# Attention kernel: both pairs of maximum products of a step issued together, behind the products of values

## The chip, the cores and the metric

The program runs on one core of a Trainium2 chip. The metric is the device time of one execution in microseconds (us), lower is better. In this text PE is TensorE's matmul stream and PEld its weight loads, DVE is VectorE, ACT ScalarE, POOL GpSimd, SP the queue engine that issues most DMAs.

## The reference

Four images of 32 x 32 tokens with 192 channels pass through two blocks. Each block adds an attention over an image's 1024 tokens (12 heads of 16 channels, with bias terms from relative positions), then a feed-forward part (routed experts in the first block; a small attention over tokens, an MLP and four experts in the second). What the change touches is the softmax attention, of which the kernel has three of the same size:

```python
attn = einsum('bnqd,bnkd->bnqk', q, k) * scale + bias     # 48 (image, head) pairs, 1024 x 1024
attn = softmax(attn, axis=-1)
out  = einsum('bnqk,bnkd->bnqd', attn, v)
```

The first two (stages c0 and c1) have the bias, the third (f1) has none.

## The kernel before, in words

`attention` (line 525) is called three times. It works through 24 pairs of heads (two heads of one image side by side), and for each pair through 8 steps, one for each tile of 128 keys. It computes scores with the keys on the partitions, so that the exponential's output can be the right operand of the product with the values. The maximum over the keys, which keeps the exponential in range, is therefore found ahead of time, by separate products with the queries on the partitions, and enters the scores as one more row of the operands. So TensorE issues, for each step of a pair:

- **scores** (`score`, line 692, matmuls at L703): for both heads, a tile of 128 keys against 1024 queries, in two matmuls of 512 columns each, into the PSUM tensors s0 and s1. ACT takes each with one exponential of 128x1024 (L996). The scores that PE issues in step n are those of key tile n; in the eighth step they are tile 0 of the next pair.
- **weigh** (line 707, matmuls at L716), the products of values, for the key tile of the step before: eight matmul records of float32, in four column groups of the array, accumulated over the eight steps in one bank. It needs the two exponentials of that tile, and these are the same two that the scores ahead of it have waited for.
- **maxima** (`use_bank`, line 660, matmuls at L688), the maximum products, for pairs ahead: four a step, as two pairs (one product of each head; the two heads lie on different rows of the array). I call the two pairs of a step A and B. Each product fills a bank of 128x512, which DVE reduces to one column (`dve_max`, L750). There are 32 products for each pair of heads; 54 are issued before the loop, the rest by a written-out plan.

Once a pair, ahead of A in step 4, stands the **row** product (L681): after the last of the 32 reductions DVE makes the negated maxima in two small operations (L755, L759), TensorE transposes them, ACT copies them out (L763), and SP's DMAs (`place_rows`, line 633) put them in place for the pair's scores.

The maximum products use three PSUM banks in turn. A product of an even number waits for both banks of its pair to be free, that is, for the reductions of the products three and two uses before it; the last of these is the first product of the previous pair. The wait and the plan are these lines:

```python
                banks = (pos, pos + 1) if item[1] % 2 == 0 else ()
            for before in (b - 3 for b in banks):
                ...
                    pe.wait_ge(*free(USES[before], pair if before >= 0 else pair - 1))
...
        for step in range(1, KT + 1):
            PLAN.append([[items.pop(0) for _ in range(2)] for _ in range(2)])
            if step == ROWS + 1:
                PLAN[-1][0].insert(0, (1, "row"))
```

The eight banks of PSUM are spent: four for the scores, three for the maxima, one for the sums. All waits are written by hand, in each engine's own stream; there is no scheduler. ACT's order is the exponentials of both heads of a tile, with the copy of the maximum row behind the first exponential of tile 4 and the copy of the sums (L1002) behind tile 0. An exponential of tile n waits for the weigh of tile n-2. In the last turn of pairs the maxima that no pair is left for are skipped: pair 22 (counted from 0) has only the first ten, pair 23 none.

Of the kernel before, what the change touches and what calls it, by code (L numbers as in the profile page):

```python
# [524 lines left out]
def attention(nc, name, vt, rel, scratch, hot, ident16, by_pool, res, wo, bo, stats=None, room=None, spots=None, spare=None,  # L525
# [6 lines left out]
    with Pool(nc, name) as m:  # L532
# [48 lines left out]
        def queries(h, version, first, count):  # L581
            at = (h * versions + version) * L + first
            return slice(at, at + count)
# [76 lines left out]
        def use_bank(pe, pair, pos, item, u, skip=()):  # L660


            started = pair is None
            g = pos if started else len(START) + len(USES) * u + pos
            if item[1] == "row":
                banks = (pos,)
            else:
                banks = (pos, pos + 1) if item[1] % 2 == 0 else ()
            for before in (b - 3 for b in banks):
                if started:  # L670
                    if before >= 0:
                        pe.wait_ge(*free(START[before], 0))
                else:
                    while before >= 0 and USES[before][0] in skip:
                        before -= 3
                    pe.wait_ge(*free(USES[before], pair if before >= 0 else pair - 1))
            bank, q = mps[g % 3], 0 if started else pair
            v = (u + item[0]) % RING
            if item[1] == "row":
                pe.wait_ge(s_m16, q + (item[0] + 1))  # L680
                ins = pe.matmul(bank[0:2 * KT, 0:P], m16[:, :], ident16, start=True, stop=True)  # L681
                ins.then_inc(s_row, 1)
            else:
                n = item[1]
                h, qi, c = n % 2, n // 4, n // 2 % 2
                rows = slice(64 * h, 64 * h + RANK)
                q0 = (c if rel else 0) * L + qi * P
                ins = pe.matmul(bank[:, :], qm[v][rows, q0:q0 + P], km[v][rows, c * CHUNK:(c + 1) * CHUNK],  # L688
                                start=True, stop=True)
                ins.then_inc(s_mm, 1)  # L690

        def score(pe, pair, u, h, kt, first=False):

            if kt == 0:
                pe.wait_ge(s_at[0], (pair + 1) * 32)
            if not first:
                pe.wait_ge(s_e, pair * 16 + (2 * kt + h - 1))
            version = kt * P // Q if rel else 0
            if rel and kt == Q // P:
                pe.wait_ge(s_at[1], (pair + 1) * (32 * (versions - 1)))  # L700
            kcol = slice(h * L + kt * P, h * L + (kt + 1) * P)
            for c in range(2):
                ins = pe.matmul(sps[h][:, c * CHUNK:(c + 1) * CHUNK], ka[u][0:R_END, kcol],  # L703
                                qa[u][0:R_END, queries(h, version, c * CHUNK, CHUNK)], start=True, stop=True)
            ins.then_inc(s_s, 1)

        def weigh(pe, pair, u, kt):

            pe.wait_ge(s_e, pair * 16 + (2 * kt + 2))
            if kt == 0:  # L710
                pe.wait_ge(s_vs, pair * 2 + 2)
                pe.wait_ge(s_o, pair + 1)
            for h in range(2):
                for c in range(2):
                    row = 32 * (2 * h + c)
                    ins = pe.matmul(ops[row:row + 32, :], vs[u][:, (h * KT + kt) * 32:(h * KT + kt + 1) * 32],  # L716
                                    pr[h][kt % 2][:, c * CHUNK:(c + 1) * CHUNK], start=kt == 0, stop=kt == KT - 1)
            ins.then_inc(s_pv, 1)

        def pe_pair(pe, turn, pair, u, skip=()):  # L720

            pos = 0

            def maxima(steps):
                nonlocal pos
                for item in steps:
                    if item[0] not in skip:
                        if item == (2, 0):
                            pe.wait_ge(s_lm[(u + 2) % RING], (turn + (u + 2) // RING + 1) * (16 * MAX_LOADS) + CONST)
                        use_bank(pe, pair, pos, item, u, skip)  # L730
                    pos += 1

            for step in range(1, KT + 1):
                if step < KT:
                    for h in range(2):
                        score(pe, pair, u, h, step)
                elif 1 not in skip:
                    pe.wait_ge(s_ld[(u + 1) % RING], (turn + (u + 1) // RING + 1) * (16 * LOADS) + CONST)
                    for h in range(2):
                        score(pe, pair + 1, (u + 1) % RING, h, 0)  # L740
                maxima(PLAN[step - 1][0])
                weigh(pe, pair, u, step - 1)
                maxima(PLAN[step - 1][1])

        def bank_of(u, item):
# [114 lines left out]
        with nc.Block() as block:  # L860
# [72 lines left out]
            @block.tensor  # L933
            def _(pe):
                pe.wait_ge(s_ones, ONES)
                pe.wait_ge(s_lm[0], 16 * MAX_LOADS + CONST)
                for pos, item in enumerate(START):
                    if item == (1, 0):
                        pe.wait_ge(s_lm[1], 16 * MAX_LOADS + CONST)
                    use_bank(pe, None, pos, item, 0)  # L940
                pe.wait_ge(s_ld[0], 16 * LOADS + CONST)
                score(pe, 0, 0, 0, 0, first=True)
                score(pe, 0, 0, 1, 0, first=True)
                with pe.Fori(0, LAST) as it:
                    for u in range(RING):
                        pe_pair(pe, it, it * RING + u, u)
                for u in range(RING):
                    pe_pair(pe, LAST, LAST * RING + u, u, LATE[u])
                project(pe)
# [1300 lines left out]
```

## Time and profile before

| | us |
|---|---|
| runs shown, median of 3 | 3374.49 |
| lowest and highest | 3373.45, 3380.55 |
| the profiled execution, its own time | 3370.78 |
| its span, first to last instruction | 3368.9 |
| PE busy in the span | 2764.8 (82%) |
| DVE busy | 2414.6 (72%) |
| ACT busy | 1860.7 (55%) |

The span and the execution's own time differ by 1.9 us. The three attentions' loops fill roughly 240 to 767, 1434 to 1961 and 2190 to 2707 us of the span; the rest is normalization, projections and feed-forward. Busy time of PE counts from a matmul's start to its modelled end, so that overlapping matmuls hide gaps in the issue; to read how closely TensorE's work follows itself, start times are compared instead.

### The profile page before, as it was taken

How to read it: one execution, taken by the hardware profiler on the slowest of the kernel's cores; microseconds unless marked ns; L12 is line 12 of the kernel's file. 1: busy time of each engine (PE TensorE's matmuls, PEld its weight loads, DVE VectorE, ACT ScalarE, POOL GpSimd, SP SyncE). 2: the span in 40 equal slices, each digit the busy share in tenths (PEclk: the TensorE clock that was granted, in tenths of full speed). 3: DMA queues.
4: the chain of work that ended last, by engine and by line, in shares of the span. 5: the costliest groups of instructions: out<-in, count | busy, mean ns of one | idle time of the engine just before them, and what ended most of it. 6: DMA issues, size and time to landing. Idle time of an engine off the chain costs nothing. (4 is left out here: it accounts for less than half of the span.)

```text
span 3368.9 us, 62705 instructions
## 1 busy us (share of the span) xinstructions
PE 2764.8 (82%) x18708; PEld 1277.7 (38%) x18708; DVE 2414.6 (72%) x4597; ACT 1860.7 (55%) x2592; POOL 435.2 (13%) x513
## 2 busy tenths in 40 slices
PE   5948999997499239589999956199999959599999
PEld 3612222226499126222222234022222236366666
DVE  6458999974766354579999955589999835465665
ACT  4416777773255124167777736067777736465554
POOL 0010111111333510101111110201111100000000
PEclk9759999996699667599999977599999979699999
DMA  2555776664122214567766701101111110200000
GB/s 64 169 125 114 151 148 142 148 126 143 33 78 76 70 31 146 134 110 150 149 146 149 145 22 50 57 28 52 48 48 49 48 32 1 55 22 5 9 5 14
DMA packets 202070, 277.27 MB, mean 82 GB/s; under 512 B 54302, under 2 KB 93454, under 8 KB 201930
## 3 DMA queue, kind: packets, MB, share of 16 engines
q1 hardware_dynamic: 162346, 211.32, 27.1%
q0 software_dynamic: 19920, 31.57, 4.0%
q10 hardware_dynamic: 19664, 32.60, 3.3%
q8 instruction: 77, 1.26, 0.2%
q14 instruction: 63, 0.52, 0.1%
HBM read 196.93 MB, written 77.46 MB: 81 GB/s over the span
## 5 line engine op out<-in xcount | busy, mean ns | idle before, releaser
L750 DVE TENSOR_REDUCE c1att_mx<-c1att_m 128x1 f32<-128x512 f32 x768 | 493.4, 685 | 35.7 <-PE c1att_m L688 30.6
L750 DVE TENSOR_REDUCE c0att_mx<-c0att_m 128x1 f32<-128x512 f32 x768 | 493.4, 685 | 32.5 <-PE c0att_m L688 27.2
L750 DVE TENSOR_REDUCE f1att_mx<-f1att_m 128x1 f32<-128x512 f32 x768 | 493.3, 685 | 26.5 <-PE f1att_m L688 21.8
L996 ACT ACTIVATE c1att_p<-c1att_s 128x1024 f32<-128x1024 f32 x384 | 373.9, 1020 | 152.0 <-PE c1att_s L703 151.9
L996 ACT ACTIVATE c0att_p<-c0att_s 128x1024 f32<-128x1024 f32 x384 | 373.9, 1020 | 148.8 <-PE c0att_s L703 148.7
L996 ACT ACTIVATE f1att_p<-f1att_s 128x1024 f32<-128x1024 f32 x384 | 373.9, 1020 | 143.8 <-PE f1att_s L703 142.8
L1426 ACT ACTIVATE moe_h<-moe_u,moe_bu 128x512 f32<-128x512 f32 x192 | 136.5, 711 | 175.6 <-PE moe_u L1343 93.9
L688 PE MATMUL f1att_m<-f1att_km,f1att_qm 16*128 16x512 f16 x768 | 155.7, 401 | 88.6 <-DVE f1att_ka L959 52.9
L716 PE MATMUL f1att_o<-f1att_p,f1att_vs 128*32 128x512 f32 x1536 | 206.2, 609 | 0.6 <-ACT f1att_p L996 0.6
L716 PE MATMUL c0att_o<-c0att_p,c0att_vs 128*32 128x512 f32 x1536 | 206.2, 609 | 0.6 <-ACT c0att_p L996 0.6
L716 PE MATMUL c1att_o<-c1att_p,c1att_vs 128*32 128x512 f32 x1536 | 206.1, 609 | 0.6 <-ACT c1att_p L996 0.6
L688 PE MATMUL c1att_m<-c1att_km,c1att_qm 64*128 64x512 f16 x768 | 156.2, 402 | 58.0 <-DVE c1att_mx L750 35.0
L688 PE MATMUL c0att_m<-c0att_km,c0att_qm 64*128 64x512 f16 x768 | 156.3, 403 | 57.7 <-DVE c0att_mx L750 34.8
L703 PE MATMUL f1att_s<-f1att_qa,f1att_ka 113*128 113x512 f16 x768 | 202.7, 385 | 0.8 <-ACT f1att_p L996 0.4
L1356 PE MATMUL moe_y<-moe_dh,xt 128*128 128x192 f16 x1536 | 195.1, 246 | 0.0
L1463 DVE TENSOR_TENSOR xt<-moe_h,xt 128x512 f16<-128x512 f32 x192 | 131.3, 691 | 86.3 <-ACT xt L1428 85.3
L1356 PE MATMUL moe_y<-moe_dl,xt 128*128 128x192 f16 x768 | 188.9, 246 | 0.0
L688 PEld LDWEIGHTS f1att_m<-f1att_km,f1att_qm 16*128 16x128 f16 x768 | 37.3, 92 | 322.6 <-DVE f1att_mx L750 264.3
L688 PEld LDWEIGHTS c1att_m<-c1att_km,c1att_qm 64*128 64x128 f16 x768 | 37.8, 93 | 292.3 <-DVE c1att_mx L750 262.4
L688 PEld LDWEIGHTS c0att_m<-c0att_km,c0att_qm 64*128 64x128 f16 x768 | 37.8, 93 | 291.7 <-DVE c0att_mx L750 262.2
L703 PE MATMUL c1att_s<-xt,c1att_ka 113*128 113x512 f16 x512 | 135.7, 387 | 7.6 <-DMA xt<-c1att_mrow 7.1
L1356 PEld LDWEIGHTS moe_y<-moe_dh,xt 128*128 128x128 f16 x1536 | 139.0, 98 | 3.7
(608 smaller groups left out, 5430.8 us busy)
## 6 DMA issues: line engine op xcount, KB each, us to landing
xt<-rel_parts SPq DMA_DIRECT2D x256, 128.0 KB, 5.0
xt<-qk_parts SPq DMA_DIRECT2D x192, 128.0 KB, 4.4
y<-rel_parts SPq DMA_DIRECT2D x128, 128.0 KB, 5.6
y<-qk_parts SPq DMA_DIRECT2D x96, 128.0 KB, 5.1
c0att_qm<-rel_parts SPq DMA_DIRECT2D x144, 64.0 KB, 2.1
c1att_qm<-rel_parts SPq DMA_DIRECT2D x144, 64.0 KB, 2.1
expert_rows<-y SPq DMA_DIRECT2D x39, 192.0 KB, 2.0
o_sums<-c0att_o ACTq DMA_DIRECT2D x24, 256.0 KB, 4.3
```

The costliest lines, as they stand in the source:

```text
L688: ins = pe.matmul(bank[:, :], qm[v][rows, q0:q0 + P], km[v][rows, c * CHUNK:(c + 1) * CHUNK], start=True, stop=True)
L703: ins = pe.matmul(sps[h][:, c * CHUNK:(c + 1) * CHUNK], ka[u][0:R_END, kcol], qa[u][0:R_END, queries(h, version, c * CHUNK, CHUNK)], start ...
L716: ins = pe.matmul(ops[row:row + 32, :], vs[u][:, (h * KT + kt) * 32:(h * KT + kt + 1) * 32], pr[h][kt % 2][:, c * CHUNK:(c + 1) * CHUNK], ...
L750: dve.tensor_reduce(mx[:, n:n + 1], bank[:, :], AX.X, ALU.max).then_inc(s_mx, 1)
L996: act.activation(pr[h][kt % 2][:, :], sps[h][:, :], ACT.Exp).then_inc(s_e, 1)
L1356: ins = pe.matmul(yps[q % 2][t // 2][:, (t % 2) * C:(t % 2 + 1) * C], hidden[q % 2][:, x], down[:, w], start=k == 0 and i == 0, stop=k == ...
L1426: act.activation(h32[:, i % 2 * CHUNK:(i % 2 + 1) * CHUNK], bank[:, :], ACT.Gelu, bias=bias, scale=1.0 / W_SCALE).then_inc(s_h32, 1)
L1463: dve.tensor_tensor(hl[q % 2][:, cols], h32[:, i * CHUNK:(i + 1) * CHUNK], hh[q % 2][:, cols], ALU.subtract).then_inc(s_hl, 1)
```

## The change

The change swaps two lines of `pe_pair`. Before, a step's order on TensorE was scores, A, weigh, B; now it is scores, weigh, A, B. In step 4 the row product, which belongs to A's list, moves behind weigh with it. No instruction is added or removed, and no wait's value changes.

```diff
@@ -738,8 +738,8 @@
                     pe.wait_ge(s_ld[(u + 1) % RING], (turn + (u + 1) // RING + 1) * (16 * LOADS) + CONST)
                     for h in range(2):
                         score(pe, pair + 1, (u + 1) % RING, h, 0)
+                weigh(pe, pair, u, step - 1)
                 maxima(PLAN[step - 1][0])
-                weigh(pe, pair, u, step - 1)
                 maxima(PLAN[step - 1][1])
```

## Rows read from the trace of the kernel before

**Rows 1.** Stretches of c0's and f1's steady loops: length, busy times, granted clock, DMA share, GB/s
```profile
276.20:742.00 465.80, 452.68 (x2770) 114.80 (x2768) 448.38 (x735) 346.01 (x386) 63.73 (x94) 1.00 0.68 142
...
2201.00:2684.00 483.00, 469.27 (x2872) 118.37 (x2869) 464.11 (x762) 358.57 (x401) 64.59 (x95) 1.00 0.17 47
```

**Rows 2.** Waits of 300 to 700 us: who for whom, us in total, times, longest
```profile
PEld c0att_m L688 <- DVE c0att_mx L750: 192.2, 294, 1.0
...
DVE c0att_mx L750 <- PE c0att_m L688: 9.2, 19, 0.5
```

**Rows 3.** Timeline, one step: start us, length us, instructions merged [idle before <- releaser]
```profile
399.69 0.39 PE L688 MATMUL c0att_m<-c0att_km,c0att_qm 64*128 64x512 f16 x2
...
400.01 1.06 PE L716 MATMUL c0att_o<-c0att_p,c0att_vs 128*32 128x512 f32 x8
...
401.01 0.10 PEld L688 LDWEIGHTS c0att_m<-c0att_km,c0att_qm 64*128 64x128 f16 x2 [0.84 <-DVE c0att_mx L750]
...
401.33 1.04 PE L703 MATMUL c0att_s<-xt,c0att_ka 113*128 113x512 f16 x4
...
402.05 1.94 ACT L996 ACTIVATE c0att_p<-c0att_s 128x1024 f32<-128x1024 f32 x2 [0.67 <-PE c0att_s L703]
402.30 0.10 PEld L688 LDWEIGHTS c0att_m<-c0att_km,c0att_qm 64*128 64x128 f16 x2 [0.42 <-DVE c0att_mx L750]
```

**Rows 4.** Timeline of the last pair, which has no maximum products: weigh, then scores
```profile
750.04 1.06 PE L716 MATMUL c0att_o<-c0att_p,c0att_vs 128*32 128x512 f32 x8
...
751.04 0.11 PEld L703 LDWEIGHTS c0att_s<-y,c0att_ka 113*128 113x128 f16 x2 [0.84 <-ACT c0att_p L996]
```

**Rows 5.** Timeline cut fine, so that single reductions and what they release show
```profile
401.43 0.69 DVE L750 TENSOR_REDUCE c0att_mx<-c0att_m 128x1 f32<-128x512 f32 x1
...
402.04 0.68 DVE L750 TENSOR_REDUCE c0att_mx<-c0att_m 128x1 f32<-128x512 f32 x1
...
437.27 0.68 DVE L750 TENSOR_REDUCE c0att_mx<-c0att_m 128x1 f32<-128x512 f32 x1
...
438.01 0.39 PE L688 MATMUL c0att_m<-c0att_km,c0att_qm 64*128 64x512 f16 x2 [0.59 <-DVE c0att_mx L750]
...
438.43 0.69 DVE L750 TENSOR_REDUCE c0att_mx<-c0att_m 128x1 f32<-128x512 f32 x1 [0.48 <-PE c0att_m L688]
```

**Rows 6.** Timeline ahead of that pair of maxima: the fourth step, with the row product
```profile
436.23 1.04 PE L703 MATMUL c0att_s<-y,c0att_ka 113*128 113x512 f16 x4
...
436.56 0.17 DVE L759 TENSOR_SCALAR c0att_m<-c0att_m 128x16 f16<-128x16 f32 x1
...
437.20 0.22 PE L681 MATMUL c0att_m<-ident,c0att_m 128*16 128x128 f16 x1
```

**Rows 7.** ACT's copy of the maximum row, once a pair of heads: count, durations, first and last start
```profile
L763 ACT ACTIVATE c0att_mrow<-c0att_m x21: 249/249/250, 285.7 to 720.4; 16x128 f16<-16x128 f32 x21
...
L763 ACT ACTIVATE f1att_mrow<-f1att_m x21: 249/249/250, 2227.6 to 2661.8; 16x128 f16<-16x128 f32 x21
```

**Rows 8.** TensorE's waits for DMAs in the first pairs of c0 and c1
```profile
PE c0att_s L703 <- DMA xt<-c0att_mrow: 4.3, 1, 4.3
...
PE c0att_m L688 <- DMA c0att_qm<-rel_parts: 2.2, 1, 2.2
...
PE c1att_s L703 <- DMA xt<-c1att_mrow: 7.1, 1, 7.1
```

**Rows 9.** c0's run-in, as a stretch (columns of rows 1), then timeline lines behind it
```profile
203.60:241.80 38.20, 16.15 (x53) 3.51 (x53) 33.44 (x54) 1.55 (x2) 10.98 (x7) 0.50 0.61 105
...
240.69 0.13 PEld L688 LDWEIGHTS c0att_m<-c0att_km,c0att_qm 64*128 64x128 f16 x2 [1.32 <-DVE c0att_mx L750]
...
242.15 0.14 PEld L688 LDWEIGHTS c0att_m<-c0att_km,c0att_qm 64*128 64x128 f16 x2 [1.32 <-DVE c0att_mx L750]
...
247.29 0.20 PEld L716 LDWEIGHTS c0att_o<-c0att_p,c0att_vs 128*32 128x32 f32 x8 [0.44 <-issue]
...
249.07 0.10 PEld L688 LDWEIGHTS c0att_m<-c0att_km,c0att_qm 64*128 64x128 f16 x2 [1.57 <-DVE c0att_mx L750]
```

## The prediction

> **What bounds the kernel now.** I read the stretches first, then the waits, then the timeline of single steps, because the first two name two different engines. In the steady loop PE is busy 97% of the time and DVE 96%, ACT 74%, at a granted clock of 1.00, which is the 2.4 GHz level [rows 1]. The waits say that DVE holds TensorE up: of 400 us, weight loads of maximum products wait 192.2 us for reductions, and DVE waits for TensorE only 9.2 us [rows 2]. One would conclude that DVE is the bound and that TensorE has room. The timeline says otherwise, and this decides the forecast.
>
> One step is 2.61 us, from A at 399.69 to the next A at 402.30 [rows 3]. In starts: A to weigh 0.32, weigh to B 1.00, B to scores 0.32, scores to the next A 0.97. Now look for what each could have waited for. The last pair of heads has no maxima at all, and there weigh is followed by scores after 751.04 - 750.04 = 1.00 us, the same [rows 4]. Scores are followed by the row product after 437.20 - 436.23 = 0.97, and that product's own input was finished at 436.56 + 0.17 = 436.73, long before [rows 5, 6]. So 1.00 and 0.97 are TensorE's own lengths for weigh and scores, with the change from one kind of matmul to the next in them. The reductions release in time: a reduction ends at 437.27 + 0.68 = 437.95 and the pair that it frees starts at 438.01, a hand-over of 0.06 [rows 5]; the reduction that frees A at 402.30 ended at 401.43 + 0.69 = 402.12, which is 0.18 before. The profile calls a gap of loads a wait for the last semaphore it sees; here the four parts 0.32 + 1.00 + 0.32 + 0.97 are TensorE's own and fill the step. **TensorE is the bound**, and DVE only just keeps up beside it, because weigh lies between A and B and scores between B and A. The pairs come 1.3 us apart, and 1.3 us is what two reductions take.
>
> Once a pair of heads the balance breaks: at the row product the three banks shift by one, A must wait for B's last reduction, and DVE then stands for 0.48 us [rows 5]. ACT's row copies are (720.4 - 285.7)/20 = 21.74 us apart in c0, (2661.8 - 2227.6)/20 = 21.71 in f1 [rows 7]; c1 repeats c0. Eight steps are 20.88, so the row product's step costs 0.85 more.
>
> **The change, part by part.** No work is added; weigh's eight records, the row product and four maximum products are only reordered. SP's and POOL's queues are not moved past anything.
>
> *Weigh ahead of A.* Its wait is for the same two exponentials that the scores before it have waited for, so it costs no new wait. Its sums and its release of ACT's buffers come 0.32 us sooner, which nothing needs: ACT already stands 0.67 us in each step for the scores [rows 3].
>
> *B directly behind A.* This is the cost. B waits for the reduction of A's first product. From the rows: A starts at 438.01 and DVE at 438.43, so 0.42; the reduction takes 0.69; the hand-over 0.06 [rows 5]. A to B becomes 0.42 + 0.69 + 0.06 = 1.17 us, in which TensorE has nothing else in its stream, where the 0.32 + 1.00 before were filled with weigh. The run-in, where pairs follow each other with nothing between, shows this loop, at a clock of 0.50: 242.15 - 240.69 = 1.46, with TensorE idle for most of it [rows 9]. So the cost lies between 1.17 (the warm parts) and 1.46 (cold whole), and not below 1.17, since each part is a measured latency; I take 1.17, as the loop's clock is 1.00.
>
> *The rest of the step.* B to scores 0.32, scores to weigh 0.97, weigh to the next A 1.00, all from rows 3. While these 2.29 us run, DVE finishes: its first reduction starts at 0.42, the second 0.61 later [rows 5], B's first at 0.42 + 0.61 + 0.61 to 0.69 (B's product is there at 1.17 + 0.42 = 1.59), B's second 0.61 later, ended near 3.0. The next A starts at 1.17 + 2.29 = 3.46 and finds all banks free. DVE then stands about 0.9 us a step. So the new step is 3.46 us against 2.61: **+0.85**. ACT needs 1.94 in it and is further from binding.
>
> *The row product's step.* DVE's two small operations (the second ends at 436.73 [rows 6]) now lie in time in which it stands anyway, and A's wait for B's last reduction, ended at about 3.4, is over when TensorE arrives at 3.46 plus the row product. What is left is the row product itself: row product to A, unhindered, is in no row. It is bounded by 0.06 and 0.32 (a whole pair with its change); I take 0.20. The extra of this step goes from 0.85 to 0.20: -0.65. ACT's copy of the row comes later, at about 3.8, and pushes the second exponential to an end near 5.1; the scores that need it start near 5.6, so nothing waits.
>
> *How often.* Pairs 0 to 21 have 8 full steps, pair 22 has two and then only an A: 178 steps. 178 x 0.85 = 151.3, less 22 x 0.65 = 14.3: 137 us for each attention, **411 us** for three. The last pairs and the run-in don't change.
>
> *Waits at the start.* In c0 TensorE waits 2.2 and 4.3 us for loads in its first pair, in c1 as much or more (7.1) [rows 8]; f1 doesn't. These loads arrive at times that TensorE's pace doesn't set. The first wait, after three steps, is covered by the 2.5 us that TensorE will be late; the second by what has gathered by then, some 3 us. About 5.5 us for each of c0 and c1 (bounds 0 and 9): -11.
>
> **Sum:** 411 - 11 = +400. The profiled execution, at 3370.8, would be 3371 + 400 = 3771; the median shown is 3.7 above it, so 3774.5 by the median.
>
> *The clock, a rule that speaks against the change.* The row product's step is a rehearsal of the new one: it is 2.61 + 0.85 = 3.46 us long with one step's work and stops of TensorE of up to 0.59 us in it [rows 5], and the clock stayed 1.00 through all of c0 and f1 [rows 1]. Now every step is so, without fuller ones between. I take the clock to stay. The Trainium skill, "TensorE: Matmul & The Clock Gate", section "A second HAM failure mode: psum-queue depth-cycling", says that a kernel cycling through PSUM banks, whose TensorE idles briefly between groups of matmuls, can swing between the half and the full clock; no stretch of this trace shows such swinging from the bank waits, and the rival below prices it.
>
> **The rivals.**
>
> *The clock swings.* At the 1.2 GHz level a step would be 1.46 for A to B [rows 9], twice 0.32, twice 0.97, and 1.78 for weigh (249.07 - 247.29 [rows 9]): 5.8 us. If half of the steps ran so, (5.8 - 3.46)/2 x 534 = +625 more: 4400; the ends are 3774 (none) and about 5020 (all). For it: TensorE stands 0.85 us in every step. Against it: rows 1, and 2.3 us of solid work in each step. Chance 0.07.
>
> *TensorE has more room than I read.* If the changes between kinds of matmul (0.32 for a pair against 0.22 of columns, about 0.1 each) are really waiting for DVE, as the profile's labels have it, the new step is shorter by three of them, 3.15: +0.54. 534 x 0.54 = 288, less 43 for the row products and 11: 3608. Against it: the equal lengths in rows 4 and 6, where no reduction is waited for. Chance 0.10.
>
> *Faster.* If B could follow A at once, the new order would save one change of kind of matmul in each step (three instead of four, 0.1 x 534 = 53 us) and the row product's waits (66 x 0.65 = 43): 3278. This holds if the bank that B's second product takes were free at A's end, that is, if DVE's backlog were under one product; it decides at the point where A to B is 0.3 and not 1.17. The code's wait and rows 5 and 9 are against it. Chance 0.03.
>
> *The order doesn't matter.* If TensorE's queue let weigh run past a waiting B, or DVE were the true bound with time to spare, nothing would change: 3374. In the row product's step TensorE did not let weigh past the waiting A (idle 0.59 [rows 5]). Chance 0.02.
>
> **How the numbers follow.** The forecast has 0.78. Its own ends: 3740 (the row step and the start better, 0.05 us less a step), 3860 (the hand-over 0.12 instead of 0.06 as cold, 32 us; nothing absorbed, 11; the row product at its upper bound, 8; 0.06 a step for the scores' issue behind a blocked B, 32). The range goes down to 3600 to take in the second rival, and up to 3870. Below and above it stay the clock and the two rivals at 3374 or faster, 0.12, and some of the forecast's own tail. Faster by over 0.2% (what a measurement of this kernel can tell from no change): 0.03; within 0.2%: 0.02; slower: 0.95.
>
> **What the changed profile would show.** Right: in the timeline, A to B 1.17 us, B to scores 0.32, scores to weigh 0.97, weigh to A 1.00; ACT's row copies about 27.9 us apart (8 x 3.46 + 0.20); a new wait of DVE for TensorE of about 0.9 us in each step, and DVE near 75% busy in the loop; granted clock 1.00; the row product's step hardly longer than others. Wrong: a clock under 1.00 between 300 and 700 us; weigh to A under 1.00 (the changes of kind would have been waits); A to B far from 1.17; a step under 3.2.

## The result, and the profile after

The changed kernel takes 3785.64 us in the median of four runs (3780.20 to 3795.49) against 3375.21 for the kernel before (3373.45 to 3380.55): 1.1216 times, with a 95% interval of 1.1188 to 1.1245. The profiled execution took 3782.08 us, 411.3 more than the 3370.78 of before; the forecast was 400 more. In medians, 3774.5 us was forecast and 3785.6 measured.

The steady loop again, as a stretch (columns as in rows 1), and the waits of the same stretch (as in rows 2):

```profile
300.00:700.00 400.00, 309.52 (x1859) 77.26 (x1860) 294.01 (x495) 234.16 (x259) 43.61 (x64) 1.00 0.56 116
```

```profile
PEld c0att_m L688 <- DVE c0att_mx L750: 216.4, 231, 1.1
...
DVE c0att_mx L750 <- PE c0att_m L688: 105.0, 115, 1.1
PE c0att_m L688 <- DVE c0att_mx L750: 90.8, 116, 0.8
```

PE has gone from 97% of the loop to 77%, DVE from 96% to 74%, ACT from 74% to 59%: no engine is full any more. What reads as a wait of weight loads for DVE grew little over [rows 2], 192.2 us to 216.4 though there are fewer of them. The telling line is the last one, which read so in the same stretch of the kernel before:

```profile
PE c0att_m L688 <- DVE c0att_mx L750: 11.2, 19, 0.6
```

Now the matmul stream itself stands for DVE 116 times, 0.78 us each. And DVE stands for TensorE 115 times. Each waits for the other in every step, which is what a loop between two engines looks like when neither has other work inside it.

One step in the timeline, to be held against [rows 3]:

```profile
404.05 0.39 PE L688 MATMUL c0att_m<-c0att_km,c0att_qm 64*128 64x512 f16 x2 [0.78 <-DVE c0att_mx L750]
404.38 1.04 PE L703 MATMUL c0att_s<-y,c0att_ka 113*128 113x512 f16 x4
405.34 1.07 PE L716 MATMUL c0att_o<-c0att_p,c0att_vs 128*32 128x512 f32 x8
406.34 0.39 PE L688 MATMUL c0att_m<-c0att_km,c0att_qm 64*128 64x512 f16 x2
406.76 1.89 DVE L750 TENSOR_REDUCE c0att_mx<-c0att_m 128x1 f32<-128x512 f32 x3 [0.98 <-PE c0att_m L688]
407.51 0.39 PE L688 MATMUL c0att_m<-c0att_km,c0att_qm 64*128 64x512 f16 x2 [0.78 <-DVE c0att_mx L750]
```

B at 404.05, scores 0.33 later, weigh 0.96 after that, A 1.00 later, the next B 1.17 after A: 3.46 us from B to B. DVE had been idle for 0.98 us when A's first reduction came at 406.76. ACT's row copies, which answer to [rows 7], in c0 and in f1:

```profile
L763 ACT ACTIVATE c0att_mrow<-c0att_m x21: 266/266/266, 292.0 to 847.6; 16x128 f16<-16x128 f32 x21
...
L763 ACT ACTIVATE f1att_mrow<-f1att_m x21: 266/266/266, 2508.0 to 3067.5; 16x128 f16<-16x128 f32 x21
```

They are (847.6 - 292.0)/20 = 27.78 us apart in c0 and 27.98 in f1, where 27.9 was forecast. That f1 is slower than c0, though it has less to load, was not forecast; the section on the small operation below comes back to it. In the step with the row product, which comes once a pair of heads, the order is weigh, row product, A:

```profile
401.85 1.07 PE L716 MATMUL c0att_o<-c0att_p,c0att_vs 128*32 128x512 f32 x8
402.73 0.22 PE L681 MATMUL c0att_m<-ident,c0att_m 128*16 128x128 f16 x1
402.88 0.39 PE L688 MATMUL c0att_m<-c0att_km,c0att_qm 64*128 64x512 f16 x2
```

### The profile page after: what moved, and what is told of

It reads as the page before. It is cut to its first block and busy times, and to the rows that moved or that the text cites. A ratio compares the mean times of both kernels' runs of the same rounds, so it can differ in the third digit from the quotient of the medians.

```text
span 3780.4 us, 62705 instructions
## 1 busy us (share of the span) xinstructions
PE 2792.5 (74%) x18708; PEld 1276.9 (34%) x18708; DVE 2381.8 (63%) x4597; ACT 1866.5 (49%) x2592; POOL 435.2 (12%) x513
## 5 line engine op out<-in xcount | busy, mean ns | idle before, releaser
L750 DVE TENSOR_REDUCE c1att_mx<-c1att_m 128x1 f32<-128x512 f32 x768 | 480.8, 684 | 179.9 <-PE c1att_m L688 179.7
L750 DVE TENSOR_REDUCE c0att_mx<-c0att_m 128x1 f32<-128x512 f32 x768 | 480.7, 684 | 176.7 <-PE c0att_m L688 176.4
L750 DVE TENSOR_REDUCE f1att_mx<-f1att_m 128x1 f32<-128x512 f32 x768 | 480.7, 683 | 176.7 <-PE f1att_m L688 176.4
```

Of the source, the lines that this page charges most:

```text
L750: dve.tensor_reduce(mx[:, n:n + 1], bank[:, :], AX.X, ALU.max).then_inc(s_mx, 1)
```

## The experiments

Every run stands beside runs of the kernel before on the same chip; ratios are against those. Medians taken on different chips differ by some microseconds for the same kernel (3370.74 to 3377.58 for the kernel before), so that small differences between runs are read from the ratios.

### The mirror: weigh last

```diff
                 maxima(PLAN[step - 1][0])
-                weigh(pe, pair, u, step - 1)
                 maxima(PLAN[step - 1][1])
+                weigh(pe, pair, u, step - 1)
```

> Order scores, A, B, weigh: the mirror of the change, weigh last instead of second. Theory (A and B side by side expose the loop product, reduction, next pair, 1.17 us, in which TensorE has nothing to do): scores to A 0.97, A to B 1.17, B to weigh 0.32, weigh to scores 1.00, a step of 3.46 us as in the changed kernel, about 3785 us. Rival (the loss comes from weigh standing ahead of the maxima, which then come late in the step): weigh last gives it back, near 3375 us.

Measured: 3775.01 us, 1.1205 (1.1188 to 1.1222). That agrees with the change's 1.1216 within the intervals: weigh's place ahead of or behind the maxima doesn't matter; that A and B lie side by side does. The timeline is the same sequence turned round:

```profile
401.74 0.39 PE L688 MATMUL c0att_m<-c0att_km,c0att_qm 64*128 64x512 f16 x2 [0.78 <-DVE c0att_mx L750]
402.06 1.06 PE L716 MATMUL c0att_o<-c0att_p,c0att_vs 128*32 128x512 f32 x8
403.05 1.04 PE L703 MATMUL c0att_s<-y,c0att_ka 113*128 113x512 f16 x4
404.02 0.39 PE L688 MATMUL c0att_m<-c0att_km,c0att_qm 64*128 64x512 f16 x2
405.20 0.39 PE L688 MATMUL c0att_m<-c0att_km,c0att_qm 64*128 64x512 f16 x1 [0.78 <-DVE c0att_mx L750]
```

### Halved reductions in both kernels

The reductions see half of each bank, so that a reduction takes 0.42 instead of 0.69 us. This leaves half of the keys out of the maxima, and the exponential takes a scale of 0.125 to stay finite.

```diff
-            dve.tensor_reduce(mx[:, n:n + 1], bank[:, :], AX.X, ALU.max).then_inc(s_mx, 1)
+            dve.tensor_reduce(mx[:, n:n + 1], bank[:, 0:CHUNK // 2], AX.X, ALU.max).then_inc(s_mx, 1)
...
-                    act.activation(pr[h][kt % 2][:, :], sps[h][:, :], ACT.Exp).then_inc(s_e, 1)
+                    act.activation(pr[h][kt % 2][:, :], sps[h][:, :], ACT.Exp, scale=0.125).then_inc(s_e, 1)
```

On the kernel before:

> The kernel before, each reduction over 256 of the 512 columns (this leaves out half of the keys from the maxima, and the exponential takes a scale of 0.125 to stay finite). Theory (TensorE is the bound of the loop before): the ordinary step stays 2.61 us; only the row product's step loses its wait, some 0.7 us x 66 = 46, and the run-in's 27 pairs x 0.27 x 3 = 22: about 3305 us. Rival (DVE is the bound, as the profile's waits name it): reductions of 0.42 instead of 0.69 us let the step fall towards TensorE's pure columns, 2.2 us: about 3375 - 534 x 0.4 - 68 = 3090 us.

On the changed kernel:

> The changed kernel with the same halved reductions (half of the keys left out of the maxima, exponential with a scale of 0.125). Theory: A to B is 0.42 + 0.42 + 0.06 = 0.90 instead of 1.17 us, the rest of the step unchanged, 3.19 us; 534 x 0.27 = 144 and the run-in's 22 less: about 3620 us. Here, and not in the kernel before, a reduction's length is in every step. Rival (the added time is TensorE's own, for instance a dearer change from weigh to maxima): A to B hardly moves, about 3765 us.

Measured: 3306.39 us (0.9811, 0.9796 to 0.9826) for the kernel before, 3612.50 us (1.0723, 1.0707 to 1.0739) for the changed one. So 0.27 us less in each of 2304 reductions gave the kernel before 64 us, and the changed kernel, by the ratios (1.1216 less 1.0723), 166. Both are close to what was expected, 68 and 166. First the kernel before with halved reductions, from its timeline the products A of two steps in a row:

```profile
399.75 0.39 PE L688 MATMUL c0att_m<-c0att_km,c0att_qm 64*128 64x512 f16 x2
...
402.36 0.39 PE L688 MATMUL c0att_m<-c0att_km,c0att_qm 64*128 64x512 f16 x2
```

and its steady loop as a stretch, columns as in rows 1:

```profile
300.00:700.00 400.00, 400.00 (x2457) 101.86 (x2459) 240.10 (x653) 307.27 (x343) 60.54 (x86) 1.00 0.70 151
```

The step is still 2.61 us, with DVE now 60% busy (240.10 of 400): DVE was not the bound of the ordinary step, in spite of 96% busy and of its name in the list of waits. The pair of heads fell from 21.7 to 21.0 us, which is eight times 2.61 and 0.15 for the row product. Then the changed kernel with halved reductions:

```profile
406.74 0.39 PE L688 MATMUL c0att_m<-c0att_km,c0att_qm 64*128 64x512 f16 x2
407.64 0.39 PE L688 MATMUL c0att_m<-c0att_km,c0att_qm 64*128 64x512 f16 x2 [0.52 <-DVE c0att_mx L750]
407.97 1.04 PE L703 MATMUL c0att_s<-xt,c0att_ka 113*128 113x512 f16 x4
408.93 1.06 PE L716 MATMUL c0att_o<-c0att_p,c0att_vs 128*32 128x512 f32 x8
409.93 0.39 PE L688 MATMUL c0att_m<-c0att_km,c0att_qm 64*128 64x512 f16 x2
```

A to B went from 1.17 to 0.90, by the length that the reduction lost, and nothing else in the step moved: 0.33, 0.96 and 1.00 as before, a step of 3.19 us.

### One pair between the scores of the two heads

```diff
-                if step < KT:
-                    for h in range(2):
+                for h in range(2):
+                    if step < KT:
                         score(pe, pair, u, h, step)
-                elif 1 not in skip:
-                    pe.wait_ge(s_ld[(u + 1) % RING], (turn + (u + 1) // RING + 1) * (16 * LOADS) + CONST)
-                    for h in range(2):
+                    elif 1 not in skip:
+                        if h == 0:
+                            pe.wait_ge(s_ld[(u + 1) % RING], (turn + (u + 1) // RING + 1) * (16 * LOADS) + CONST)
                         score(pe, pair + 1, (u + 1) % RING, h, 0)
-                maxima(PLAN[step - 1][0])
+                    if h == 0:
+                        maxima(PLAN[step - 1][0])
                 weigh(pe, pair, u, step - 1)
                 maxima(PLAN[step - 1][1])
```

> Order scores of head 0, A, scores of head 1, weigh, B. Theory (any two pairs must lie 1.17 us apart, the loop product, reduction, hand-over, whatever fills the time): A to B is 0.32 + 0.54 + 1.00 = 1.86 us, B to the next A would be 0.32 + 0.54 = 0.86 by TensorE's own work and is held to 1.17: a step of 3.03 us, +0.42 x 534 = 224, less about 16 at the row products: 3583 us. Rival (only products side by side hurt, or only the number of changes of kind counts): one change more in each step, +0.1 x 534: 3430 us.

Measured: 3578.06 us (1.0591, 1.0575 to 1.0607). B, half of the scores, and A:

```profile
400.60 0.39 PE L688 MATMUL c0att_m<-c0att_km,c0att_qm 64*128 64x512 f16 x2
400.92 0.61 PE L703 MATMUL c0att_s<-xt,c0att_ka 113*128 113x512 f16 x2
401.77 0.39 PE L688 MATMUL c0att_m<-c0att_km,c0att_qm 64*128 64x512 f16 x2 [0.24 <-DVE c0att_mx L751]
402.09 0.60 PE L703 MATMUL c0att_s<-xt,c0att_ka 113*128 113x512 f16 x2
402.62 1.07 PE L716 MATMUL c0att_o<-c0att_p,c0att_vs 128*32 128x512 f32 x8
403.62 0.39 PE L688 MATMUL c0att_m<-c0att_km,c0att_qm 64*128 64x512 f16 x2
```

B itself and half of the scores are 0.86 us of TensorE's work, the two pairs are still 1.17 apart, and the stop has shrunk to 0.24 (in the matmul stream). With three banks the smallest distance between any two pairs is 1.17 us; a step costs what the order leaves of it uncovered. In the kernel before, the distances were 1.32 and 1.29, both above it.

### More banks, in both orders

Four rotating banks and one more for the row product, taken from the scores: the two halves of a head's scores go to one bank, the second over the first, so half of the scores is left out. The exponential reads that bank twice, which keeps ACT's work the same. The main lines:

```diff
-        sps = [m.ps(f"s{h}", L) for h in range(2)]
-        mps = [m.ps(f"m{k}") for k in range(3)]
+        sps = [m.ps(f"s{h}") for h in range(2)]
+        mps = [m.ps(f"m{k}") for k in range(4)]
+        rowps = m.ps("row")
...
-            for before in (b - 3 for b in banks):
+            for before in (b - 4 for b in banks):
...
-                ins = pe.matmul(sps[h][:, c * CHUNK:(c + 1) * CHUNK], ka[u][0:R_END, kcol],
+                ins = pe.matmul(sps[h][:, :], ka[u][0:R_END, kcol],
```

> The changed kernel's order with four rotating banks for the maxima and a fifth of its own for the row product. The banks come from the scores: the two halves of a head's scores go to one bank, the second over the first, and the exponential reads that bank twice (this leaves out half of the scores, at the same work for TensorE and ACT). Theory (the missing fourth bank is the whole cause): B follows A after 0.2 to 0.3 us, TensorE's step is 2.5 us and DVE's four reductions of 0.65 set 2.6; a pair of heads takes about 21.1 us, the kernel about 3330 us, faster than before. Rival (weigh ahead of the maxima or the side-by-side order is slow by itself): a step stays over 3 us, 3600 to 3785 us.

> The kernel before with the same five banks (same scores left out): the control to the run beside it. Theory: the ordinary step stays at TensorE's 2.61 us, since no bank was waited for in it; only the row product's step loses 0.7 us: a pair of heads 21.0 to 21.1 us, about 3330 us, the same as the changed order within 15 us. Rival (the kernel before waited for banks in each step too, as the profile's waits say): clearly under 3300 us.

Measured: the changed order 3350.73 us (0.9914, 0.9899 to 0.9929), the order before 3316.17 us (0.9813, 0.9798 to 0.9828). With the same banks in both, the distance between the two orders falls from 410 us to 34.6, so the bundled order costs what it does because the banks are three. The two orders are not equal, though, where I had allowed 15 us, and the changed order is 20 us above its expected 3330. In c0's steady loop a pair of heads takes 21.5 us in the changed order and 21.0 in the order before. Two of the changed order's steps show why:

```profile
400.25 0.31 PEld L686 LDWEIGHTS c0att_m<-c0att_km,c0att_qm 64*128 64x128 f16 x4 [0.84 <-DVE c0att_mx L750]
400.79 0.11 PEld L701 LDWEIGHTS c0att_s<-xt,c0att_ka 113*128 113x128 f16 x2 [0.23 <-issue]
...
402.76 0.10 PEld L686 LDWEIGHTS c0att_m<-c0att_km,c0att_qm 64*128 64x128 f16 x2 [0.84 <-DVE c0att_mx L750]
403.22 0.10 PEld L686 LDWEIGHTS c0att_m<-c0att_km,c0att_qm 64*128 64x128 f16 x2 [0.37 <-DVE c0att_mx L750]
403.54 0.11 PEld L701 LDWEIGHTS c0att_s<-xt,c0att_ka 113*128 113x128 f16 x2 [0.23 <-ACT c0att_p L997]
```

At 400.25 four loads of the maxima follow at once, and the step from A to A is 402.76 - 400.25 = 2.51 us: there the order does save one change of kind of matmul. In the next step B must wait until 403.22: DVE's reductions of a burst of four start 0.60 us apart, from 400.68 on, and the last one, of the previous B's second bank, ends at 403.17. Of the steps between 300 and 700 us B follows A after 0.22 us in half, and after 0.46 or 0.88 in most others; the mean step is 2.69 us, against 2.63 in the order before. Even with a fourth bank, pairs spread evenly are the better order here.

### The row product elsewhere

The step with the row product costs 0.85 us more in the kernel before. This edit takes the row product out of the rotation: it goes into head 1's score bank, between head 0's scores and A. The main lines:

```diff
-            bank, q = mps[g % 3], 0 if started else pair
+            bank, q = sps[1] if item[1] == "row" else mps[g % 3], 0 if started else pair
...
+                if step == ROWS + 1 and 1 not in skip:
+                    score(pe, pair, u, 0, step)
+                    pe.wait_ge(s_e, pair * 16 + 2 * step)
+                    use_bank(pe, pair, 0, (1, "row"), u, skip)
+                    maxima(PLAN[step - 1][0])
+                    pe.wait_ge(s_qm, pair + 2)
+                    score(pe, pair, u, 1, step)
+                    weigh(pe, pair, u, step - 1)
+                    maxima(PLAN[step - 1][1])
+                    continue
```

> The kernel before, with the row product taken out of the rotation of the three banks: it goes into head 1's score bank, between head 0's scores and A of step 4, and ACT copies it ahead of that step's exponentials. Theory: the step with the row product costs 3.03 instead of 3.46 us (one more change of kind 0.1, row product 0.15, a wait of 0.16 for ACT's copy), 0.43 x 66 = 28 less: about 3347 us, faster than before. Rival (the row product's step is dear by its own transpose and copy, not by the shifted banks): no gain, 3375 us or a little more for ACT's later exponentials.

Measured: 3370.20 us, 0.9995 (0.9986 to 1.0004): no gain. I had counted only TensorE's side. The chain in the trace goes through DVE:

```profile
437.05 0.17 DVE L764 TENSOR_SCALAR c0att_m<-c0att_m 128x16 f16<-128x16 f32 x1
437.16 2.48 DVE L755 TENSOR_REDUCE c0att_mx<-c0att_m 128x1 f32<-128x512 f32 x4
...
437.90 0.10 PEld L683 LDWEIGHTS c0att_m<-c0att_km,c0att_qm 64*128 64x128 f16 x2 [0.54 <-DVE c0att_mx L755]
```

A waits until 437.90 for B's first reduction, which began at 437.16 because DVE's two small operations stood ahead of it. With the shift of banks gone, the small operations themselves were next; the run with both edits, below, bears that out.

### One small operation fewer

DVE's second small operation (the negation) goes: the reduction writes float16, and ACT's copy takes the sign. The buffer of maxima is tripled, so that DVE need not drain ahead of its next write.

```diff
-            dve.tensor_reduce(m32[:, :].rearrange("p (h q) -> p h q", h=2),
+            if not isinstance(pair, int) or pair:
+                dve.wait_ge(s_m16, pair)
+            dve.tensor_reduce(m16[:, :].rearrange("p (h q) -> p h q", h=2),
                               mx[:, :].rearrange("p (q c h) -> p h q c", c=2, h=2),
-                              AX.X, ALU.max).then_inc(s_chain, 1)
-            dve.wait_ge(s_chain, pair + 1)
-            dve.tensor_scalar(m16[:, :], m32[:, :], -1.0, None, ALU.mult).then_inc(s_m16, 1)
+                              AX.X, ALU.max).then_inc(s_m16, 1)
...
-            act.activation(mrow[u][:, :], bank[0:2 * KT, 0:P], ACT.Copy).then_inc(s_qm, 1)
+            act.activation(mrow[u][:, :], bank[0:2 * KT, 0:P], ACT.Identity, scale=-1.0).then_inc(s_qm, 1)
```

On the kernel before:

> The kernel before, with DVE's second small operation gone: the final reduction writes float16 itself, and ACT's copy of the row takes the sign (scale -1); three buffers of maxima in turn, so that DVE need not drain. Theory (once a pair of heads, A waits for a reduction that stands behind these small operations): 0.22 us x 66 = 15 less, about 3358 to 3360 us. Rival (that step is bound elsewhere): no change, 3371 to 3375 us.

On the kernel with the row product elsewhere:

> Both single edits together on the kernel before: row product in head 1's score bank, and DVE's second small operation gone. In the run with the bank alone, A of step 4 waited for a reduction that stood behind DVE's small operations; theory: with one of them gone that wait is 0.22 us shorter, 66 x 0.22 = 15 less than that run: about 3357 us against 3375, some 6 below the run with the operation alone gone. Rival (the order with split scores is now held by ACT's copy): no better than the run with the operation alone gone, 0.9956 of before.

On the changed kernel:

> The changed kernel without DVE's second small operation. Theory (in the changed order DVE stands about 0.9 us a step, so its small operations cost nothing): where the same edit gave 0.22 us a pair of heads to the kernel before, here a pair of heads stays at 27.72 us; what is left to win is the rare hit in which that operation lasts 2.1 to 2.2 us instead of 0.17 beside a POOL instruction (two of 72 in the profiled run, one of them followed by a fall of the clock to 0.50 for 6.8 us): 0 to 8 us, 3777 to 3785. Rival (the edit helps here as much as before): 15 us.

And the changed kernel as it is, beside it:

> The changed kernel again, beside the run without the small operation. Theory: 1.1216 times the kernel before within 0.003, 3780 to 3795 us; the profile again shows nearly all pairs of heads at 27.7 us, and any longer one beside a small operation of DVE of about 2 us that overlaps a POOL instruction. Rival (the long pairs are TensorE's or a DMA's): long pairs without such an operation.

Measured: the kernel before with the edit 3363.27 us, 0.9956 (0.9942 to 0.9969); with the row product elsewhere as well 3360.08 us, 0.9950 (0.9936 to 0.9963); the changed kernel with the edit 3769.97 us, 1.1164 (1.1149 to 1.1179), and without it 3784.86 us, 1.1211 (1.1196 to 1.1226). So the edit gives about 15 us to either kernel, and makes the kernel before 0.4% faster, which the interval tells from no change. That gain is the forecast 0.22 us a pair of heads (21.69 us before, 21.48 with the edit, in most pairs of the profile). To the kernel with the row product elsewhere it gives the forecast 15 us (0.9995 to 0.9950), but whether both edits together beat this one alone, by the 6 us that were expected, the intervals don't tell. On the changed kernel I had expected 0 to 8, since there DVE's small operations lie in idle time, and the steady pair indeed stays as it was. So the 15 us come from somewhere else. The changed kernel as it is came out as expected, and once its loops are steady its long pairs of heads lie beside long executions of that operation.

The operation's 72 executions in the changed kernel's second run, grouped by attention (shortest/median/longest in ns):

```profile
L759 DVE TENSOR_SCALAR c0att_m<-c0att_m x24: 174/174/2345, 229.7 to 875.6; 128x16 f16<-128x16 f32 x24
L759 DVE TENSOR_SCALAR c1att_m<-c1att_m x24: 174/175/2239, 1561.3 to 2207.1; 128x16 f16<-128x16 f32 x24
L759 DVE TENSOR_SCALAR f1att_m<-f1att_m x24: 174/174/2232, 2448.7 to 3095.4; 128x16 f16<-128x16 f32 x24
```

and one of the long ones in the timeline of that run:

```profile
2841.36 2.35 POOL L924 TENSOR_TENSOR f1att_t<-f1att_t 96x1024 f32<-96x1024 f32 x1 [4.98 <-DMA f1att_t<-rz_rows]
2841.38 0.19 DVE L755 TENSOR_REDUCE f1att_m<-f1att_mx 128x16 f32<-128x32 f32 x1
2841.60 2.14 DVE L759 TENSOR_SCALAR f1att_m<-f1att_m 128x16 f16<-128x16 f32 x1
...
2843.80 0.22 PE L681 MATMUL f1att_m<-ident,f1att_m 128*16 128x128 f16 x1 [0.64 <-DVE f1att_m L759]
```

An operation on 16 columns takes 2.14 us and ends (2843.74) where POOL's product, begun 0.24 us before it, ends (2843.71). The small reduction beside the same POOL instruction, 0.19 us, is not held up. I call such a long execution a hit on the negation. It goes by the order of the starts: in the profiles of the changed kernel (two) and of the mirror, all seven negations that start within this POOL instruction end with it, and the five that start 0.03 to 0.16 us ahead of it take 0.17 us. So this hits when POOL's work, set off once in three pairs of heads by a DMA, falls onto the negation. In the kernel before it never was longer than 289 ns in the profiled run; in the changed kernel it was hit twice in the first profiled run and four times in this one. The stretch behind the hit shows the second price, the granted clock (the figure ahead of the DMA share, third from the right):

```profile
2836.00:2846.00 10.00, 6.21 (x39) 1.49 (x35) 7.88 (x11) 5.01 (x6) 4.68 (x4) 1.00 0.12 40
2846.20:2849.60 3.40, 3.40 (x14) 0.68 (x14) 1.71 (x3) 1.93 (x2) 1.53 (x3) 0.53 0.24 60
2850.00:2900.00 50.00, 38.18 (x233) 9.44 (x229) 36.12 (x60) 28.37 (x31) 2.87 (x7) 1.00 0.12 35
```

TensorE had stood 0.64 us ahead of the row product and 0.97 ahead of A, beside the usual 0.78 ahead of each B, and then ran for 3.4 us at the lower of the clock's two levels. The fall doesn't always follow. In the mirror one negation was hit as well:

```profile
2579.62 2.04 DVE L759 TENSOR_SCALAR f1att_m<-f1att_m 128x16 f16<-128x16 f32 x1
2581.72 0.22 PE L681 MATMUL f1att_m<-ident,f1att_m 128*16 128x128 f16 x1 [0.54 <-DVE f1att_m L759]
2582.91 0.39 PE L688 MATMUL f1att_m<-f1att_km,f1att_qm 16*128 16x512 f16 x2 [0.97 <-DVE f1att_mx L750]
```

The clock stayed at 1.00 there, and the two pairs of heads around it were 1.6 us longer in all, where the two pairs around the hit shown above were 3.5 us longer. What decides whether the clock falls, no run here shows. The changed kernel without the operation had no such fall once its loops were steady, and from the third row copy of each loop its time for a pair stayed within 27.7 to 28.0 us (27.2 for the last).

The hits do not explain all of the distance between the two profiled executions, 24.0 us: the four hits, with what follows them, make 14; 3.9 us lie at the start of c1's loop and 3.4 behind the last attention. How often the executions without a profile were hit is not known. That the hits make the 15 us between the medians is therefore likely, but not shown.

## Why the prediction was right

The mechanism holds, and so does the time, 3785.6 against 3774.5, though some of its small terms were off and partly cancel. By its steps:

- *TensorE is the bound, though the waits name DVE.* Right. Reductions shorter by 40% left the step at 2.61 us.
- *B waits for A's first reduction: 1.17 us.* Right, 1.17 in the timeline; it shrinks by just what the reduction loses; and it is the same 1.17 with other work between.
- *The rest of the step, 0.32 + 0.97 + 1.00.* Right: 0.33, 0.96, 1.00. The step is 3.46 us.
- *The row product's step, 0.20 more than the others.* Too dear. The row product starts 0.88 us after weigh (401.85 to 402.73), not 1.00, and A follows it after 0.15. A pair of heads takes 27.72 us, and 27.87 each third time: 27.77 on average, 0.11 less than forecast, or 7 us in 66 pairs.
- *The start of c0 and c1 absorbs 11 us.* The effect is there, but smaller. From the first to the last exponential of an attention, c0 grew from 521.6 to 656.7, c1 from 525.0 to 656.7, f1 from 515.4 to 655.1: +135.1, +131.7, +139.7. Without the hits on the negation (3.4 us in c0, 4.6 in f1) that is +131.7, +131.7 and +135.1, where the forecast had 131.5, 131.5 and 137. The first two lie 3.4 below the third, so the start absorbed about 7 us, not 11. The longest waits for the row shrank from 4.3 and 7.1 us to 2.2 and 3.7 and the first waits went, but in the second pair of heads the clock stood at 0.50 for 6.8 and 10.2 us, where it had stood there for 3.4 and 6.8.
- *What the sum lacked* is the hit on the negation: in f1 two pairs of heads were longer than their like by 0.8 and 3.8 us, in c0 one by 2.1, with 1.4 more behind it at the lower clock: 8 us in all. The other 5 of the 411 us lie outside the loops and have no cause shown; executions of the changed kernel differ by 15.
- Without the hits the loops grew by 398.5 us, where 400 was forecast. That it is so near is in part luck: the cheaper row step (-7) and the smaller absorption at the start (+4) pull against each other.
- *The clock stays at 1.00.* Right for the loop at large: between 300 and 700 us it is 1.00 with a stop of 0.78 us in every step. The Trainium skill, "TensorE: Matmul & The Clock Gate", section "A second HAM failure mode: psum-queue depth-cycling", speaks for the rival of a swinging clock; the trace of the steady loop doesn't agree with it. Behind a hit on the negation, though, the clock fell for 3.4 or 6.8 us.
- *TensorE has more room than I read.* This rival is out: in the changed step weigh to A is still 1.00, although DVE had finished 0.56 us before A started (it stands from 405.78 to 406.76), and with halved reductions the old step stays at 2.61.
- *The faster rival* had the right condition. With a fourth bank the changed order can run a step in 2.51 us, one change of kind less than 2.61; but then DVE's bursts are next, and it is still slower than the old order with the same banks.

## What to carry to other kernels

Before reordering, find the shortest distance that two uses of a rotating buffer can have (product 0.42, reduction 0.69, hand-over 0.06 here), and keep that much of the engine's other work between each two of them: spread beats bundled as long as the buffers are few. An engine named as the releaser of a wait isn't the bound until its length, halved, moves the time; compare start-to-start distances with a place where the wait can't exist. And a tiny operation is worth removing even where it lies in idle time, if another engine's instruction can hold it up.

## What the hardware showed that I had not expected

- DVE's `tensor_scalar` from float32 to float16 on 128x16 in SBUF, 0.17 us alone, takes 2.0 to 2.35 us when it starts within POOL's `tensor_tensor` on 96x1024 (2.35 us), ending with it; one that starts just ahead of it takes 0.17, and a `tensor_reduce` of 0.19 us within the same POOL instruction isn't held up. The Trainium skill, "SBUF — State Buffer", section "SBUF: two separate sides", says that DVE in a mode with two ports and GpSimd share one pair of ports under an exclusive lock, held for a whole instruction. The seven long executions in three profiled runs agree with it; that this operation ran in such a mode no row shows.
- A short loss can cost twice. In the hit shown above the row product came 0.83 us late and A another 1.04; the clock's fall to 0.50 for 3.4 us, which followed, makes the rest of the 3.5 us by which the two pairs of heads were longer (28.48 and 30.33 us between row copies, against 27.68 in pairs of their kind), about 1.6. In the mirror, where the clock stayed, a hit cost 1.6 in all.
- The change from one kind of matmul to another costs about 0.1 us: a pair of maximum products takes 0.32 us before scores or weigh, and 0.22 where the next is of the same kind and nothing is waited for, as in half of the steps of the changed order with four banks (a step of 2.51 us with three changes, against 2.61 with four). Why, no run here shows.
